# A decoder layer on one core: the attention's two counted loops written out as straight code

## The reference, cut to what matters

```python
x = x + attn(layernorm(x), w_q_down, w_q_up_nope, w_q_up_rope, w_kv_down, w_k_rope, w_uk, w_uv, w_out)
x = x + cross_attention(layernorm(x), ctx)
x = x + ffn(layernorm(x), k0, s0, k1, s1, k2, s2)

# attn, per head h:
q_lat  = (c_q @ w_q_up_nope[h]) @ w_uk[h]
scores = q_lat @ c_kv.T + rope(c_q @ w_q_up_rope[h]) @ rope(k).T
probs  = softmax(causal(scores / sqrt(192)))
out   += ((probs @ c_kv) @ w_uv[h].T) @ w_out[h]
```

## Time and profile before

| | |
|---|---|
| time, median of 3 runs | 1919.62 us (1919.01 to 1919.92) |
| span of the profiled execution | 1917.3 us |
| PE, share of the span busy | 100% |
| DVE | 80% |
| ACT | 61% |
| POOL | 55% |
| TensorE clock granted | 1.000 of full, throughout |
| DMA, mean | 205 GB/s |

### The profile page before, as it was taken

The page is one execution under the profiler, slowest core; times in us unless marked ns, Lnnn a source line. Parts: engine busy times, 40 slices in busy tenths (PEclk is TensorE's granted clock), DMA queues, the critical chain, the costliest instruction groups (busy, mean ns, idle before and its releaser), DMA issues.

```text
span 1917.3 us, 32648 instructions
## 1 busy us (share of the span) xinstructions
PE 1909.2 (100%) x10048; PEld 1615.0 (84%) x10048; DVE 1531.8 (80%) x2655; ACT 1168.9 (61%) x2648; POOL 1048.7 (55%) x891
## 2 busy tenths in 40 slices
PE   9999999999999999999999999999999999999999
PEld 7888888888888888888888888888888877888887
DVE  6778888888888887877777777777878889996677
ACT  5456767676758575765555555555656668766441
POOL 5468777787869696865555556555565511000000
PEclk9999999999999999999999999999999999999999
DMA  9838474647474655588546264464628286466645
GB/s 361 333 105 317 133 260 130 253 125 263 122 266 138 231 171 199 195 319 328 181 151 233 77 230 132 158 207 140 217 82 302 91 285 250 198 220 245 229 152 176
DMA packets 86473, 393.13 MB, mean 205 GB/s; under 512 B 9472, under 2 KB 10240, under 8 KB 67328
## 3 DMA queue, kind: packets, MB, share of 16 engines
q1 hardware_dynamic: 86400, 392.21, 58.0%
HBM read 236.46 MB, written 155.71 MB: 205 GB/s over the span
## 4 chain that ended last, share of the span: by engine, by line
PE 97%; DVE 2%; DMA 1%; ACT 0%; issue 0%; DVEq 0%; POOL 0%; ACTq 0%; SPq 0%
PE at_out L1281 11%; PE at_out L1285 10%; PE at_out L1282 10%; PE at_qbank L55 7%; PE at_qbank L57 7%; PE at_qbank L56 7%; PE at_score L1244 6%; PE at_score L1235 3%; PE at_turned L1256 3%; PE at_qbank L1605 3%; PE at_score L1605 2%; PE at_out L1605 2%; PE at_value L56 2%; PE at_value L55 2%; PE at_value L57 2%; PE at_qbank L1608 2%
## 5 line engine op out<-in xcount | busy, mean ns | idle before, releaser
L2620 DVE TENSOR_TENSOR at_acc<-at_out,at_acc 128x512 f32<-128x512 f32 x640 | 438.9, 689 | 138.2 <-PE at_out L1285 136.2
L2266 POOL TENSOR_TENSOR at_acc<-at_stage,at_acc 128x512 f32<-128x512 f32 x256 | 332.3, 1298 | 184.1 <-ACT at_stage L1747 174.5
L1281 PE MATMUL at_out<-at_wvo,at_val_hi 128*128 128x512 f32 x896 | 365.3, 408 | 0.5 <-ACT at_stage L1747 0.2
L1285 PE MATMUL at_out<-at_wvo,at_val_lo 128*128 128x512 f32 x896 | 350.6, 391 | 0.0
L1282 PE MATMUL at_out<-at_wvo,at_val_hi 128*128 128x512 f32 x896 | 350.5, 391 | 0.0
L1747 ACT ACTIVATE at_stage<-at_out 128x512 f32<-128x512 f32 x256 | 153.0, 599 | 125.2 <-PE at_out L1285 112.9
L1787 ACT ACTIVATE at_pT_hi<-at_turned 128x512 fp32r<-128x512 f32 x128 | 76.4, 597 | 245.8 <-PE at_turned L1256 245.8
L2226 POOL TENSOR_TENSOR at_probs<-at_probs,at_row_stats 128x512 f32<-128x512 f32 x128 | 133.3, 1041 | 148.2 <-DVE at_row_stats L2582 148.2
L1781 ACT ACTIVATE at_probs<-at_probs,at_row_stats 128x128 f32<-128x128 f32 x512 | 197.7, 388 | 8.8 <-DVE at_row_stats L2577 8.8
L1285 PEld LDWEIGHTS at_out<-at_wvo,at_val_lo 128*128 128x128 f32 x896 | 168.4, 188 | 37.8
L1281 PEld LDWEIGHTS at_out<-at_wvo,at_val_hi 128*128 128x128 f32 x896 | 169.1, 189 | 31.1 <-DVE at_acc L2620 5.7
(11 more groups left out here) (313 smaller groups left out, 4772.3 us busy)
## 6 DMA issues: line engine op xcount, KB each, us to landing
parts_d<-at_rope_tmp SPq DMA_DIRECT2D x32, 1024.0 KB, 6.1
at_qrope<-parts_d SPq DMA_DIRECT2D x128, 256.0 KB, 5.3
wvo_d<-at_wvo SPq DMA_DIRECT2D x16, 2048.0 KB, 7.8
at_wvo<-wvo_d SPq DMA_DIRECT2D x16, 2048.0 KB, 8.1
ff_w_d<-ff_w SPq DMA_DIRECT2D x21, 1024.0 KB, 6.2
ff_w<-ff_w_d SPq DMA_DIRECT2D x21, 1024.0 KB, 4.8
ab_raw<-in_w_heads SPq DMA_DIRECT2D x32, 576.0 KB, 5.5
wvo_d<-at_wvo SPq DMA_DIRECT2D x16, 1024.0 KB, 9.8
```

The lines of the kernel that those rows point to most:

```text
L1281: pe.matmul(out, hi, weight[:, 0], start=start, stop=False, skip_group_check=True)
L1285: pe.matmul(out, lo, weight[:, 0], start=False, stop=True, skip_group_check=True).then_inc(out_ready, 1)
L2266: pool.tensor_tensor(at, stage[group][z][:], at, ALU.add).then_inc(pool_added, 1)
L2620: dve.tensor_tensor(at, outb[FACTORS[name][2]][:], at, ALU.add).then_inc(added, 1)
```

## The change

All four loops are unrolled when the program is built: the two in `quads` and the two of SP. The quad number is then a Python integer. The engines do the same matmuls, vector operations and DMAs in the same order; branches and register arithmetic of the loops are gone, every count waited for is a constant, and the program holds 13 quads' worth of code where it held 2, on four engines (11 where it held 2 on SP).

```diff
@@ quads, called by PE, ACT, POOL and DVE
             for s in range(STEPS):
                 slot(0, s, 2 * STEPS, "full", first_use(0))
-            with eng.Fori(1, QUADS - 1) as q:
+            for q in range(1, QUADS - 1):
                 for s in range(STEPS):
                     slot(q, s, 2 * STEPS, "full", first_use(q))
             for s in range(STEPS):
                 slot(QUADS - 1, s, 2 * STEPS, "switch", first_use(QUADS - 1))
-            with eng.Fori(QUADS, 2 * QUADS - 1) as q:
+            for q in range(QUADS, 2 * QUADS - 1):
                 for s in range(STEPS):
                     slot(q, s, 2 * STEPS, "later", first_use_later(q))
@@ SP
             full_quad(0)
-            with sp.Fori(1, QUADS - 2) as q:
+            for q in range(1, QUADS - 2):
                 full_quad(q)
             full_quad(QUADS - 2, then_later=True)
             switch_quad(QUADS - 1)
             later_quad(QUADS, 1, first=True)
-            with sp.Fori(QUADS + 1, 2 * QUADS - 1) as m:
+            for m in range(QUADS + 1, 2 * QUADS - 1):
                 later_quad(m, m - (QUADS - 1))
```

## The result

| | before | after |
|---|---|---|
| time, median of 20 runs each | 1919.37 us (1918.47 to 1922.44) | 1922.78 us (1921.35 to 1923.48) |
| ratio, 95% interval | | 1.0016 (1.0009 to 1.0023) |
| span of the profiled execution | 1917.3 us | 1920.5 us |

The change makes the kernel a little slower: +3.4 us between the medians, +3.2 us between the spans. The whole interval lies above 1.000. By size it is just inside the 0.2% (3.8 us) that the prediction took as no change. The predicted time was 1920.7, the range 1918.4 to 1922.9: it holds the result near its upper end. The +1.1 us of the sum is a third of what came.

The account below looks back on a forecast made before the run. PE was taken to bound the kernel, so only delays reaching it count. Step 7's +0.9 us and steps 2 to 6's +0.2, all else 0, made +1.1: from 1919.6 to 1920.7 us, range 1918.4 to 1922.9.

Parts of the forecast that it names:

- What bounds the kernel: Whole kernel: PE is nearly always busy, so only time PE loses can be won and only delays reaching PE cost.
- Branches, register arithmetic: Loop branches and sequencer arithmetic: removing them gains 0, as queued work covers them; branches fully exposed would be 2.3 us.
- Constant counts, step 7: Quads 1 to 6: second constant waits delay two DVE adds about 0.07 us each, reaching PE; +0.15 a quad, +0.9 us.
- Steps 2 to 6: Quads 1 to 6: at most +0.08 us a quad, half taken; +0.2 us, with ends 0 and +0.5.
- Steps 0 and 1: Quads 1 to 6, without a written-out twin: taken as 0, chain unchanged; ends -1.9 and +0.9 us.
- Group 1: Second loop's quads: added DVE delays covered by slack, since the written-out switch quad keeps 9.36 us steps; 0.
- D: Rival: instruction fetches of the longer code show; four exposed packets give +3.8 us, all 44 +53, 1972 us; chance 0.04.
- Fetching: Longer program: some 44 more instruction packets on PE's queue, taken as 0; upper end +0.5 us.
- The range: Upward the terms' upper bounds, +2.8 us, plus 0.5 for run spread; downward it takes in B.
- A: Rival: each of eleven taken branches makes PE fetch again, so the change wins 13 us, 1906.4 us; chance 0.03.
- B: Rival: no delay reaches PE, as step 7's are eaten by something earlier; 0 to -1 us, 1919.2 us; chance 0.16.
- C: Rival: two DVE delays in each of group 0's 48 steps all reach PE; +7.2 us, 1926.8 us; chance 0.05.

Follow-up runs that it names:

- e11: e3, with the late wait of PE's rope matmuls in step 1 also put ahead of the early one: 1918.44 us, ratio 0.9994.
- e8: The kernel before, loops kept, DVE's two waits turned round only in the written-out quads 0, 7 and 15: 1918.28 us, ratio 0.9994.
- e3: The changed kernel with the order of DVE's two waits turned round before P6's add and the fifth add: 1918.30 us, ratio 0.9997 against before.
- e5: The changed kernel with the two waits turned round before DVE's fifth add only: 1920.14 us, ratio 1.0004 against before.
- e6: The changed kernel with the two waits turned round before DVE's P6 add only: 1920.22 us, ratio 1.0001 against before.
- e7: e3, with the double waits of ACT's copies to the stage and POOL's adds from it turned round too: 1919.17 us, ratio 0.9997.
- e4: The kernel before, loops kept, with DVE's two waits turned round before P6's add and the fifth add everywhere: 1919.42 us, ratio 0.9999.
- e10: The kernel before with only PE's two quad loops written out: 1920.28 us, ratio 1.0004.
- e9: The changed kernel with further, long-fulfilled waits adding a semaphore instruction before DVE's P6 add and fifth add: 1933.67 us, ratio 1.0072 against before.

## Why the prediction was right and wrong, by its steps

**What bounds the kernel:** right. Only what reaches PE changed the time, and distances between PE's starts told it; the busy shares moved by about 0.1 point at most.

**Branches, register arithmetic:** right, 0. Straight code with its hops turned away (e11) and loops (before, e8) have the same quads to 0.03 us, 92.06 against 92.07 and 92.09, and the same 83.04.

**Constant counts, step 7:** right in mechanism and size: +0.155 us each in six quads, +0.9. e3 takes it away by order alone, e5 and e6 halve it. The chain named is the last of three that carry the hops to PE in this step; the waits for the banks that the adds free, which the prediction left out, come ahead of it and shift by 0.08 and 0.15.

**Steps 2 to 6:** +0.04 us a quad by measurement, +0.2, as taken. Here the agreement is partly luck: e3 and e7, equal in these steps' hops on DVE, differ by 0.03 us there.

**Steps 0 and 1:** the step that failed. The text took 0 "because no double wait with a computed count stands between `turn` and L2532". That was true of the wait it looked at, L2532's, which did not move, but another wait of PE ends in the same step: the rope matmuls' for the bank that L2537 frees. Its chain comes from `value_sums`, which stands on DVE behind both adds, and runs on over ACT's `latent` copy. The text had named `value_sums` among what stands behind the waiting add, and then wrote that PE waits for the last two of the three only. Two hops there give +0.15 us; PE's own double wait gives 0.05 more, which the earlier trace rows could not show and the list of the double waits in front of critical matmuls would have. Step 1 measured +0.207 us, six times: +1.24 us, over the upper end of +0.9 too. Step 0 gave +0.03 a quad, +0.2.

**Group 1:** the second term that failed: taken as 0, measured +1.21 us. The argument, that the switch quad has the hops and keeps its 9.36 us, was one quad long, and it does not carry over: behind quads with the hops the same quad 7 has steps of 9.376 us and more. P6's hop alone is indeed free (e5); with the fifth add's, steps take 17 ns longer (e4, e6), by a way that stays open. The quads were 83.09 to 83.28 us, 83.21 in the mean, and the prediction had said that 83.1 or more "would prove D". It would not have: e10 has the packets without the delay, and e4 has the delay in a loop.

**Fetching:** right, 0, with 42 more packets on PE's queue where 44 were estimated. The 31 more on q14, of the other engines, the prediction did not count; e3 has them too and costs nothing.

The failed terms (+1.2 and +0.2 in steps 1 and 0, +1.2 in group 1, +0.2 in quad 7, whose code is the same in both kernels and which the prediction had no term for) make +2.8 us beside the right +1.1; less the 0.7 behind quad 14, which is scatter, that is the +3.2 of the spans.

**The range** held, but not by its own reasoning. Steps 0 and 1 went over their upper end, and group 1 had none. What made room was the +0.5 each for fetching and for the spread of the runs and 0.3 not used in steps 2 to 6. Counted from the 1919.37 us of the runs beside it instead of the 1919.62 on which the range was built, +3.4 lies just outside its +3.3.

**The rivals.** A would have needed a gain; the passes of the second loop show no fetch, and e10, without PE's branches, is no faster. By the Trainium skill ("Runtime: NRT & Kernel Launch", instruction fetch mechanics) a taken branch outside the fetched window forces a fetch; no run here bears that out. With no instruction packet in rows 6, none here shows either that a branch left what was loaded. B fell with step 7. D fell with e3 and e10. C is what happened, in small: hops reached PE where slack was short, in steps 1 and 7. In e9, with more of them, steps 2 and 3 and those of group 1 follow.

## What to carry to other kernels

When a loop is written out, or a count becomes a constant, look at every instruction that waits for two things: in straight code put the wait that comes last first in program order, in a loop the other way round where both counts are computed, and the 0.05 to 0.09 us behind the late wait are gone. Then follow not one wait of PE in one step but all of them in every step, since one late engine feeds several chains. And a cost that sits in slack today is priced by the slack that is left: two hops a step cost 3.4 us, two more another 10 to 11.

## What the runs showed of the hardware that was not expected

- A second wait costs by its place: 0.075 to 0.08 us on DVE, about 0.05 on PE where the late wait stands last in straight code, nothing where it stands first (e3, e11). In a loop, with both counts computed, the late wait standing first costs 0.09 us (e4). A further semaphore instruction behind the late wait costs about 0.1 more (e9).
- 42 more instruction packets (0.7 MB over the program) cost PE nothing in group 1, where its quads stay at 83.04 us (e10), although the DMA engines are half busy there.
- Steps of 9.360 us turn to 9.377 in the quads where the fifth add has a hop of 0.075 us on DVE, with no wait shown on PE: single weight loads and matmuls, those on at_qbank above all, start a few ns later each. Once quads 1 to 6 have run with the hop, quad 7 shows it without one (e4). Why is open; no run here was made that could tell it.
- Turning the order in quads 0, 7 and 15 shortens quad 15 from 70.46 to 70.00 us in the traces (e3; 69.99 in e7). The best three versions, e3, e8 and e11, have medians 1.1 to 1.6 us under the kernel before in the same groups; all their intervals reach over 1.000, so that none is shown to be faster.
